# Two attention layers whose normalized and attended rows are turned by DMA instead of by TensorE

## The reference

```python
h = relu(layernorm(x));  x = x + L0(h, adj)      # 12-head attention over the graph's edges, with q, k, v biases
h = relu(layernorm(x));  x = x + L1(h, adj)      # directed layer: similarity, softmax, left / self / right projections
h = relu(layernorm(x));  x = x + L2(h, adj)      # two more directed layers in a row
h = relu(layernorm(x));  x = x + L3(h, adj)      # 12-head attention with an additive bias and an output projection
```

## Time and profile before

| | |
|---|---|
| median of 3 runs | 2442.68 us (2442.14 to 2443.14) |
| the profiled execution, its own time | 2443.86 us |
| its span from first to last instruction | 2441.8 us |
| mean granted TensorE clock over the span | 0.979 of full speed |
| PE busy / DVE / ACT / POOL | 96% / 81% / 76% / 67% |
| instructions | 79454 |

### The profile page before, as it was taken

The page is one execution under the profiler, slowest core; times in us unless marked ns, Lnnn a source line. Parts: engine busy times, 40 slices in busy tenths (PEclk is TensorE's granted clock), DMA queues, the critical chain, the costliest instruction groups (busy, mean ns, idle before and its releaser), DMA issues.

```text
span 2441.8 us, 79454 instructions
## 1 busy us (share of the span) xinstructions
PE 2338.5 (96%) x26448; PEld 1723.4 (71%) x26448; DVE 1979.9 (81%) x8952; ACT 1848.9 (76%) x4660; POOL 1633.8 (67%) x2194
## 2 busy tenths in 40 slices
PE   4699999999999999999999999999999999999985
PEld 3467777777777777777777777777777777777753
DVE  7768888888888888888888888888888888888863
ACT  4468777777777887877787787788778787777763
POOL 2157767767767776776777677677767777776762
PEclk8799999999999999999999999999999999999997
DMA  6113332323323233332333332232333323323221
GB/s 203 50 32 56 60 61 58 62 53 61 59 57 64 54 64 55 61 59 53 63 57 62 59 62 59 52 63 58 60 61 61 59 53 61 59 60 61 53 42 36
DMA packets 443559, 148.15 MB, mean 61 GB/s; under 512 B 410128, under 2 KB 443152, under 8 KB 443152
## 3 DMA queue, kind: packets, MB, share of 16 engines
q1 hardware_dynamic: 443152, 143.07, 29.7%
HBM read 29.76 MB, written 12.58 MB: 17 GB/s over the span
## 4 chain that ended last, share of the span: by engine, by line
PE 84%; POOL 3%; issue 3%; DMA 2%; DVE 1%; ACT 0%; SPq 0%; DVEq 0%; POOLq 0%; ACTq 0%
PE bank L147 21%; PE bank L149 21%; PE bank L148 21%; PE bank L1536 4%; PE bank L1474 4%; PE bank L1523 2%; DMA pT<-p 2%; PE bank L1430 2%; PE bank L1490 1%; PE bank L1492 1%; PE bank L1491 1%; PE bank L1581 1%; PE bank L1578 1%; PE bank L1579 1%; POOL p L632 1%
## 5 line engine op out<-in xcount | busy, mean ns | idle before, releaser
L147 PE MATMUL bank<-w_hi,dir_hT_hi 128*128 128x384 f16 x1728 | 564.5, 327 | 0.0
L148 PE MATMUL bank<-w_lo,dir_hT_hi 128*128 128x384 f16 x1728 | 564.2, 327 | 0.0
L149 PE MATMUL bank<-w_hi,dir_hT_lo 128*128 128x384 f16 x1728 | 564.1, 326 | 0.0
L764 ACT ACTIVATE probs<-minus_scores,minus_max 128x128 f32<-128x128 f32 x1536 | 488.2, 395 | 75.0 <-DVE minus_max L1017 75.0
L632 POOL TENSOR_TENSOR p<-probs,p 128x512 f16<-128x512 f32 x384 | 446.9, 1164 | 123.7 <-ACT p L771 123.6
L147 PE MATMUL bank<-hT_hi,w_hi 128*128 128x128 f16 x2304 | 401.0, 220 | 6.3 <-DVE w_lo L303 4.3
L148 PE MATMUL bank<-hT_lo,w_hi 128*128 128x128 f16 x2304 | 401.1, 221 | 0.0
L149 PE MATMUL bank<-hT_hi,w_lo 128*128 128x128 f16 x2304 | 400.9, 220 | 0.0
L1017 DVE CUSTOM_DVE_ANT_0 minus_scores<-bank,minus_score_bias 128x128 f32<-128x128 f32 x1536 | 343.3, 286 | 16.1 <-issue 13.5
L640 POOL TENSOR_TENSOR raw_weights<-raw_weights,gain_offset 128x384 f32<-128x384 f32 x192 | 192.2, 1001 | 151.7 <-ACT raw_weights L851 151.7
L148 PEld LDWEIGHTS bank<-w_lo,dir_hT_hi 128*128 128x128 f16 x1728 | 169.4, 98 | 112.6 <-issue 1.2
(11 more groups left out here) (177 smaller groups left out, 7259.8 us busy)
## 6 DMA issues: line engine op xcount, KB each, us to landing
x<-in_x SPq DMA_DIRECT2D x64, 192.0 KB, 2.6
out<-raw_weights SPq DMA_DIRECT2D x64, 192.0 KB, 2.2
pT<-p SPq DMA_TRANSPOSE x384, 3.1
adj_tile<-in_adj SPq DMA_DIRECT2D x64, 64.0 KB, 2.2
raw_weights<-in_L_gnn_Wq SPq DMA_DIRECT2D x2, 576.0 KB, 4.3
raw_weights<-in_L_gnn_Wk SPq DMA_DIRECT2D x2, 576.0 KB, 5.5
raw_weights<-in_L_gnn_Wv SPq DMA_DIRECT2D x2, 576.0 KB, 6.6
raw_weights<-in_L_gnn_Wl SPq DMA_DIRECT2D x2, 576.0 KB, 6.0
```

What stands on the lines that cost most here:

```text
L147: pe.matmul(out, stat[0], move[0], start=first, stop=False)
L148: pe.matmul(out, stat[0], move[1], start=False, stop=False)
L149: return pe.matmul(out, stat[1], move[0], start=False, stop=last)
L764: last = act.activation(probs[:, i, :], scores[:, i, :], ACT.Exp, bias=nmax[:, t.slot(), i:i + 1], scale=-1.0)
```

## The change

- `att_turn_h`, `att_turned_hi`, `att_turned_lo` are gone. In their place `att_hi` (ACT) rounds `h` to fp16 in `h16`, `att_lo` (POOL) writes the rest beside it, and `turn_h` (SP) turns both halves, 128 x 768 fp16 elements, with one DMA transpose into `hT`. `project_q` and `project_k` wait for `hT_ready`.
- `turn_o`, `turned_o_hi`, `turned_o_lo` are gone. `attended_rows` of `last` now writes its result back into `pv` in PSUM; `attended_hi` (ACT) and `attended_lo` (DVE) split it from there into `o16`, and `turn_o` (SP) turns both halves by one DMA transpose into `oT`, for which `project_out` waits.
- SP's list gets three more transposes a round. `turn_h` and `turn_o` of `last` stand ahead of the three `turn_probs` of `first`; the output of a graph is written one round later, so there are 67 rounds, and the last holds only that write.
- The lists of PE, ACT, DVE and POOL are reordered: `project_v` of `last` moves from the head of a round to the end of the one before, `combine(lower)` ahead of `dir_turn_h(single)`, `project_q` ahead of `project_k` for `last`, `q_evict` and `k_evict` of `last` behind `sides_hi(upper)`, and `part_sides(upper)` behind `add_to_x(single)` and `dir_stats(lower)`.
- To make room, `adj_tile` keeps 6 graphs instead of 8, and some tiles move to reused memory.

The diff's core (in order: sizes, the functions and lists of SP, then POOL, ACT and DVE):

```diff
-ADJ_KEPT = 8
+ADJ_KEPT = 6
-OPENED, LAST_ROUND = 1, G - 1 + 3
+OPENED, LAST_ROUND = 1, G - 1 + 4
-        hT = [sb(f"hT_{a}", [P, 2, D], F16) for a in ("hi", "lo")]
+        h16 = [sb(f"h16_{n}", [P, 2, D], F16) for n in (0, 1)]
+        hT = sb("hT", [P, 2, 2 * C, P], F16)
...
+                def turn_h(t):
...
+                    wait_apart(sp, (hT_ready, t.count(-1, 16)), (h_lo, t.count()), (v_psum, t.count(-2)))
+                    sp.dma_start_transpose(hT[:, t.slot(), :, :],
+                                           h16[t.slot()][:, :, :].rearrange("p a n -> p (a n)")).then_inc(hT_ready, 16)
+                def turn_o(t):
...
+                    wait_apart(sp, (oT_ready, t.graph_count(-1, 16)), (o_lo, t.graph_count()), (o_psum, t.graph_count(-1)))
+                    sp.dma_start_transpose(oT[:, :, :], o16[:, :, :].rearrange("p a n -> p (a n)")).then_inc(oT_ready, 16)
...
                 def step(n_):
                     turn_probs(n_.last(3), 2)
-                    load_x(n_.first(-2))
                     turn_probs(n_.last(3), 0)
                     turn_probs(n_.last(3), 1)
+                    load_x(n_.first(-2))
+                    att_load_adj(n_.first(-2))
+                    turn_h(n_.last(2))
+                    turn_o(n_.last(3))
                     turn_probs(n_.first(-1), 0)
-                    att_load_adj(n_.first(-2))
                     turn_probs(n_.first(-1), 1)
                     turn_probs(n_.first(-1), 2)
-                    write(n_.last(3))
+                    write(n_.last(4))
+                    turn_h(n_.first(-2))
...
                 W0.load_matrices(sp)
                 W1.load_matrices(sp)
+                turn_h(first[0])
                 load_beta(sp)
...
                 W1.ready(sp)
                 W2_upper.load_matrices(sp)
                 W2_upper.load_vectors(sp)
+                turn_h(first[1])
                 load_x(first[2])
...
+                def att_lo(t):
...
+                    wait(pool, h_hi, t.count())
+                    pool.tensor_tensor(h16[t.slot()][:, 1, :], h[:, :], h16[t.slot()][:, 0, :], ALU.subtract).then_inc(h_lo, 1)
...
-                def att_turned_hi(t):
...
-                    wait(act, v_psum, t.count(-2))
-                    wait(act, hT_psum, t.count())
-                    act.activation(hT[0][:, t.slot(), :], hT_bank[:, 0:D], ACT.Copy).then_inc(hT_hi, 1)
+                def att_hi(t):
...
+                    wait_apart(act, (h_ready, t.count()), (hT_ready, t.count(-2, 16)))
+                    act.activation(h16[t.slot()][:, 0, :], h[:, :], ACT.Copy).then_inc(h_hi, 1)
...
+                def attended_hi(t):
...
+                    wait(act, oT_ready, t.graph_count(-1, 16))
+                    wait(act, attended_ready, t.count())
+                    act.activation(o16[:, 0, :].rearrange("p (h e) -> p h e", h=H), pv[:, :, 0:HD], ACT.Copy).then_inc(o_hi, 1)
...
-                def att_turned_lo(t):
...
-                    wait(dve, hT_hi, t.count())
-                    dve.tensor_tensor(hT[1][:, t.slot(), :], hT_bank[:, 0:D], hT[0][:, t.slot(), :],
-                                      ALU.subtract).then_inc(hT_lo, 1)
...
+                def attended_lo(t):
...
+                    wait(dve, o_hi, t.graph_count())
+                    hi, lo = (o16[:, n, :].rearrange("p (h e) -> p h e", h=H) for n in (0, 1))
+                    dve.tensor_tensor(lo, pv[:, :, 0:HD], hi, ALU.subtract).then_inc(o_lo, 1)
```

More of the change, by code:

```diff
@@ L687, in _ @@
                 att_norm(first[0])
+                att_lo(first[0])
                 keep_biases(pool)
@@ L694, in _ @@
                 att_norm(first[1])
+                att_lo(first[1])
                 add_attended(first[0])
@@ L707, in _ @@
                 att_norm(first[2])
+                att_lo(first[2])
                 add_attended(first[1])
@@ L899, in step @@
                     left_hi(n_.lower(0))
-                    att_turned_hi(n_.first(-2))
+                    probs_hi(n_.last(2), 2)
+                    probs_hi(n_.last(2), 0)
                 att_normed(first[0])
-                att_turned_hi(first[0])
+                att_hi(first[0])
                 W0.split_high(act)
@@ L919, in _ @@
                 att_normed(first[1])
-                att_turned_hi(first[1])
+                att_hi(first[1])
                 dir_input(single[0])
@@ L945, in _ @@
                 att_normed(first[2])
+                att_hi(first[2])
                 exponent(lower[0])
                 left_hi(lower[0])
-                att_turned_hi(first[2])
                 act.wait_ge(setup, 3)
@@ L1281, in step @@
-                    part_sides(n_.upper(1))
-                    att_mean_var(n_.first(-2))
-                    v_lo_split(n_.first(-1))
-                    denominator(n_.upper(1))
-                    att_var_eps(n_.first(-2))
-                    scaled_denominator(n_.upper(1))
-                    left_lo(n_.upper(1))
-                    turned_o_lo(n_.last(3))
-                    add_to_x(n_.single(0))
-                    drop_masked(n_.first(-2))
-                    dir_stats(n_.lower(0))
+                    diagonal(n_.upper(1))
@@ L1292, in step @@
+                    att_mean_var(n_.first(-2))
+                    score_bias(n_.last(2))
+                    add_to_x(n_.single(0))
+                    dir_stats(n_.lower(0))
+                    part_sides(n_.upper(1))
                     dir_mean_var(n_.lower(0))
                     dir_var_eps(n_.lower(0))
-                    diagonal(n_.upper(1))
+                    denominator(n_.upper(1))
+                    v_lo_split(n_.first(-1))
+                    right_lo(n_.upper(1))
+                    att_var_eps(n_.first(-2))
@@ L1445, in project_q @@
                     wait(pe, max_ready[C - 1], t.count(-1))
-                    wait(pe, hT_lo, t.count())
+                    wait(pe, hT_ready, t.count(0, 16))
                     project_turned(t, 0, q_bank, q_psum)
@@ L1494, in attend @@
                         mm.then_inc(pv_psum, 1)
-                def turn_o(t):
-                    if t is None:
-                        return
-                    wait(pe, attended_ready, t.count())
-                    for c in range(C):
-                        mm = pe.transpose(oT_bank[:, c128(c)], attended[:, c128(c)], ident[:, :])
-                    mm.then_inc(oT_psum, 1)
                 def project_out(t):
@@ L1587, in step @@
                     project_k(n_.first(-1))
-                    project_v(n_.last(3))
+                    combine(n_.lower(1))
                     dir_turn_h(n_.single(0))
-                    combine(n_.lower(1))
                     project_q(n_.first(-1))
@@ L1618, in step @@
                     attend(n_.first(-1), 2)
-                    combine(n_.upper(1))
                     similarity(n_.lower(0))
                     project_left(n_.lower(0))
-                    att_turn_h(n_.first(-2))
+                    project_v(n_.last(2))
                     project_self(n_.lower(0))
```

199 lines of the change are left out of this document (93 added, 106 removed).

## The result

The changed kernel takes 2413.99 us (median of 4 runs, 2412.77 to 2419.43) against 2442.91 for the kernel before, run beside it: ratio 0.9885, 95% interval 0.9868 to 0.9902. The profiled execution took 2413.84 us, its span 2412.1.

The account below looks back on a forecast made before the run. PE's own work was taken to bound the rounds. 2443.9 - 60 (PE) + 3 (waits) + 7 (opening) + 5 (end) = 2398.9, less 1.2 for the median: 2398 us, range 2380 to 2428.

Parts of the forecast that it names:

- PE's saving: On PE, dropping three fp32 transposes a group, 185 groups at 0.325 us, saves 60 us; a round becomes 34.65 us.
- What the other engines get: Per round, DVE 28.8 us and POOL 27.3, ACT +0.03 us twice, DMA share some 0.4; no engine overtakes PE.
- The walk through a round: PE's new list summed from the round's start; turned tiles arrive in time, `hT` of `last` with 1.7 us to spare.
- The place called the tightest: ACT's `k_evict(last2)` ends at 25.5 to 26.2, score due at 26.15: from 0.65 us to spare to 0.05 late.
- +3: In the rounds, 0.05 us of new waiting each, 3 us in all; bounds 0 and 0.4 a round.
- the chain to `k_evict`: From the combine at 16.2 through POOL's `single0` work (done 22.2) and DVE's sides (24.0 to 24.7) to `k_evict` (25.5 to 26.2).
- The 1.2 us that it gave `oT`: Before `project_out(last3)`, needed at 24.7: `oT` lands by DMA at 23.5, 1.2 us to spare.
- Case 2: In the rounds, a wait of 0.4 us each, from tight hand-overs and DVE instructions stretched beside POOL: 2423 us; chance 0.14.
- Case 3: Slower or level: the chain to `k_evict(last2)` slips by one POOL instruction, 1.0 us, giving 2460 us; chance 0.09.
- Case 4: The DMA itself is late: transposes land after 7.7 us, `oT` 3.4 us late each round, 2609 us; chance 0.02.
- Case 5: Start and end of the kernel cost nothing: about 2383 us; chance 0.07.
- Start and end: Opening +7 us, graph 1's `turn_h` queued behind `W2_upper` loads (bounds 0, 9); end +5 us, nothing hiding the DMA (3, 8).

Follow-up runs that it names:

- Experiment 8: Changed kernel with graph 1's `turn_h` ahead of the `W2_upper` loads and `first`'s first `pT` transpose ahead of `last`'s `turn_h` and `turn_o`: 2398.68 us, ratio 0.9822.

## Why the prediction was right in sign and place, and 15 us too low

**PE's saving: right.** 0.325 us a group was forecast, 0.61 for two and 0.33 for the third were measured. An undisturbed round is 34.68 to 34.69 against 34.65. 576 transposes less took 61 us of PE's busy time, and 60 was the term.

**What the other engines get: right.** In the changed kernel, by line and shape:

```profile
L761 ACT ACTIVATE h<-h 128x384 f16<-128x384 f32 x128 | 67.0, 523 | 10.9 <-ACT h L755 0.4 <-issue 0.4
```

```profile
L592 POOL TENSOR_TENSOR h<-h,h 128x384 f16<-128x384 f32 x128 | 117.3, 917 | 113.3 <-ACT h L761 113.3
```

This is 523 ns against 517 and 917 against 920; DVE 28.6 us a round against 28.8, POOL 27.4 against 27.3, DMA share 0.38 to 0.40 against 0.4.

**The walk through a round: right to 0.6 us, but for the last `pT` of `first`.** SP's timeline in the round that starts at 1249.38:

```profile
1266.90 1.70 SPq L486 DMA_TRANSPOSE hT<-h  x1
1270.18 1.21 SPq L493 DMA_TRANSPOSE raw_weights_of_out<-raw_weights  x1
1271.55 4.15 SPq L499 DMA_TRANSPOSE pT<-p  x3
```

and ACT's `k_evict` of `last` in it:

```profile
1274.80 0.57 ACT L783 ACTIVATE kT<-bank,weight_unscale 128x384 f32<-128x384 f32 x1
```

`turn_h` goes out at 17.5 of the round (16.9 forecast), `turn_o` at 20.8 and lands at 23.5 (20.4 and 23.5), `project_out` starts at 24.77 (24.7), and `k_evict` ends at 25.99 (25.5 to 26.2 forecast, due at 26.15). The place called the tightest held: PE has no row of waits for `kT`. The place that did not is the last `pT` of `first`. The walk let the three go out 1.23 us apart from 21.7 on and land at 27.3, 1.8 us ahead of PE's need at 29.1. They go out 1.4 us apart from 22.2 on (the row of three takes 4.15 us), and in this round the last is issued at 25.0 and lands at 28.2. The median over the rounds is 28.9, so 0.3 us are left of 1.8.

**The failed step is the size of one term: "+3", 0.05 us of new waiting a round.** It was put on the hand-overs of the chain to `k_evict`. The waits came elsewhere: 13.0 of 16.3 us are for `pT` and `oT`, where the kernel before had 4.1. All together they are 16.3 - 4.1 = 12.2 us more, four times the term; by the means of the rounds (0.34 over the shortest after, 0.09 before) it is 0.25 us a round, about 15 us, which lies within the bounds given for it (0 to 0.4 a round). The step had two things wrong. It took a DMA's landing as one number, "one lands 3.1 us after its issue", though 3.1 is a median: in the trace of before 22 of 351 `pT` took over 4 us, and the ten waits of up to 0.7 us in the earlier trace rows were the sign of it. And it had 1.8 us to spare for the last `pT` of `first`, where `turn_o` and three `pT` in a row leave 0.3 in the median. The 1.2 us that it gave `oT` were right. Experiment 8 takes one `pT` out of that row, the last one then lands at 27.5, near the forecast, and its waits are gone, though 67 of 360 `pT` are still late.

**The rivals.** Case 2 came nearer in size, by another cause: 0.4 us a round at 2423, the truth between it and the forecast. Of its cause, DVE instructions stretched beside POOL, little is to be seen: the 12-column row that took 1138 ns now takes 1194, and no row of PE's waits names it:

```profile
L1070 DVE TENSOR_SCALAR rnorm<-rsum,weight_unscale 128x12 f32<-128x12 f32 x64 | 76.4, 1194 | 0.0
```

Case 3 did not come. Case 4, a DMA that is always late, would have cost 3.4 us a round and did not come; an `oT` that lands 1.3 us or more late in 14 of 60 rounds is its mild form. The Trainium skill, "VectorE: DVE Perf Modes", section "The three transpose paths", has 1309 ns for a 128 x 128 block by DMA. The trace disagrees with it as a cost per block: six blocks land 2.74 us after SP begins to issue them. Case 5 was wrong on both ends.

**Start and end: right.** The start came to +8.4 against +7, and moving one line took 6.8 off. At the end of the changed kernel `h` starts at 2374.28 and `hT` lands at 2379.47, 5.2 us (5.5 forecast, 2.9 before); from the end of `attended` at 2401.92 to the landing of `oT` at 2405.99 it is 4.1 (4.35 forecast, 2.1 before). In the chain that ended last:

```profile
2376.72 2.75 DMA hT<-h
...
2403.24 2.75 DMA raw_weights_of_out<-raw_weights
```

## What to carry to other kernels

Cost a transfer that PE will wait for by the upper end of its landing times, not by the median: if the slack of a tile is below the difference, each late landing above it is paid in full. A few short waits for a DMA in the trace of before are the first sign of that tail. Walk the queue that issues the transfers as you walk the busiest engine: with three transposes more in a round, 77 of 360 `pT` were late instead of 22 of 351, most of them behind another transpose. In this kernel, reordering the DMA queue was worth more than making room in PE's list: a `pT` that was ready early and stood behind a `turn_h` and a `turn_o` that were not cost 8.5 us and took one line to mend, where the one try at taking room from PE's list cost 19.

## What the hardware showed that was not expected

- Packets of two queues of the kind "instruction" run on the DMA engines while the kernel runs: 406 in the span, the long ones 16 KB and 0.9 to 1.8 us. They are 0.8% of the engines' time, and a transpose that meets one lands up to 2.3 us late for `oT` (4.99 for 2.74) and in single cases 2.8 us for `pT` (5.8 for 3.05).
- A transpose that is issued while another is under way lands a little later even when it meets no instruction packet: in the changed kernel such a `pT` takes 3.15 us in the median and up to 3.41, one issued after the transpose ahead has landed 3.04 and up to 3.06.
- The Trainium skill, "Trainium Architecture — The Big Picture", section "The software stack", has the instruction streams brought into the engines' memory when the program is loaded. The rows of the queues "instruction" show packets throughout this execution too, so what this trace has is not a load at the start alone.
- Copies of 4 rows of 16 KB ran as 16 packets of 4 KB, those of 16 rows of 32 KB as 16 packets of 32 KB, about 1.6 us each.
